# Attention's first unit on Trainium2: no strip moves, four tiles transposed on TensorE and taken off the bank by VectorE

## What is computed

```python
x = x + 0.5 * ffn(layernorm(x))
# attention of the middle part
q = layernorm(x) @ Wq.T + bq
scores = q @ memory_keys.T / sqrt(128)
probs = softmax(scores, axis=-1)
x = x + (probs @ memory_values) @ Wo.T + bo
x = x + 0.5 * ffn(layernorm(x))
```

## Time and profile before

| | |
|---|---|
| Median of 3 runs | 674.98 us (672.7 to 675.78) |
| The profiled execution | 673.04 us, span 671.4 us |
| PE, PEld busy | 613.3 us (91%), 432.9 us (64%) |
| DVE, ACT, POOL busy | 530.8 us (79%), 461.5 us (69%), 381.9 us (57%) |
| Mean granted clock of TensorE | 0.975 |
| DMA | 59.06 MB, strip moves: 480 issues |

### The profile page before, as it was taken

The page is one execution under the profiler, slowest core; times in us unless marked ns, Lnnn a source line. Parts: engine busy times, 40 slices in busy tenths (PEclk is TensorE's granted clock), DMA queues, the critical chain, the costliest instruction groups (busy, mean ns, idle before and its releaser), DMA issues.

```text
span 671.4 us, 9169 instructions
## 1 busy us (share of the span) xinstructions
PE 613.3 (91%) x2784; PEld 432.9 (64%) x2800; DVE 530.8 (79%) x968; ACT 461.5 (69%) x765; POOL 381.9 (57%) x378
## 2 busy tenths in 40 slices
PE   3888989669989999999999999999999987999997
PEld 2444434447667877778778778787787866645542
DVE  4889877858977887887897897897898765699885
ACT  3576777446667767777777786776776753577886
POOL 3856660035366766767687587586587783533100
PEclk9899999969998999999999999999999986999999
DMA  8021210043463553743734636527436320000000
GB/s 296 2 62 33 62 32 0 17 110 78 111 163 75 140 122 85 167 103 89 170 86 122 154 73 151 130 69 175 109 86 162 92 61 1 0 18 16 32 33 31
DMA packets 35555, 59.06 MB, mean 88 GB/s; under 512 B 8539, under 2 KB 9139, under 8 KB 35379
## 3 DMA queue, kind: packets, MB, share of 16 engines
q1 hardware_dynamic: 31891, 53.75, 31.8%
q10 hardware_dynamic: 3616, 4.73, 2.8%
HBM read 8.12 MB, written 2.10 MB: 15 GB/s over the span
## 4 chain that ended last, share of the span: by engine, by line
PE 62%; DVE 17%; issue 6%; ACT 4%; SPq 4%; POOL 3%; DMA 1%; ACTq 1%; DVEq 0%; POOLq 0%
PE banks L1244 7%; PE banks L1246 7%; PE banks L1245 7%; PE banks L1285 7%; PE banks L1286 6%; PE banks L1287 6%; PE banks L1264 4%; SPq L308 4%; PE banks L1120 4%; DVE probsT L895 3%; PE banks L1129 3%; DVE bank_max L998 3%; DVE E L993 3%; PE banks L1136 3%; PE banks L1295 2%
## 5 line engine op out<-in xcount | busy, mean ns | idle before, releaser
L460 POOL TENSOR_TENSOR p_lo<-probsT,p_hi 128x768 fp32r<-128x768 f32 (+1 forms) x128 | 226.7, 1776 | 174.7 <-ACT p_hi L652 174.5
L998 DVE TENSOR_REDUCE bank_max<-banks 128x1 f32<-128x1024 f32 x128 | 156.2, 1220 | 36.5 <-PE banks L1246 35.4
L652 ACT ACTIVATE p_hi<-probsT 128x768 fp32r<-128x768 f32 (+1 forms) x128 | 104.5, 816 | 22.9 <-PE banks L1287 18.9
L1244 PE MATMUL banks<-kv_lo,q_parts 128*128 128x512 f32 x256 | 112.6, 440 | 7.3 <-ACT E L670 4.8
L559 ACT ACTIVATE probsT<-probsT 128x1024 bf16<-128x1024 bf16 x96 | 92.2, 980 | 34.5 <-DVE probsT L895 31.6
L993 DVE STREAM_TRANSPOSE E<-E 128x1024 f32<-128x1024 f32 x92 | 113.6, 1234 | 2.1 <-ACT E L670 2.1
L895 DVE SCALAR_TENSOR_TENSOR probsT<-banks,E 128x1024 bf16<-128x1024 f32 x80 | 95.5, 1217 | 22.5 <-PE banks L1120 20.6
L1285 PE MATMUL banks<-p_hi,kv_lo 128*128 128x512 f32 x256 | 110.0, 430 | 2.5 <-POOL p_lo L460 2.1
L670 ACT ACTIVATE E<-banks,neg_max 128x1024 f32<-128x1024 f32 x92 | 102.4, 1113 | 7.4 <-DVE neg_max L1004 4.6
L644 ACT ACTIVATE p_hi<-banks 128x256 fp32r<-128x256 f32 (+1 forms) x128 | 52.3, 409 | 78.5 <-PE banks L1264 78.3
L1286 PE MATMUL banks<-p_lo,kv_hi 128*128 128x512 f32 x256 | 104.0, 406 | 0.0
(11 more groups left out here) (110 smaller groups left out, 880.3 us busy)
## 6 DMA issues: line engine op xcount, KB each, us to landing
probsT<-E SPq DMA_DIRECT2D x248, 128.0 KB, 2.4
probsT<-E SPq DMA_DIRECT2D x168, 64.0 KB, 2.0
E<-in_keys_values SPq DMA_DIRECT2D x8, 512.0 KB, 3.5
probsT<-E ACTq DMA_DIRECT2D x56, 64.0 KB, 2.4
out<-X SPq DMA_DIRECT2D x8, 256.0 KB, 2.1
X<-in_x SPq DMA_DIRECT2D x1, 1280.0 KB, 9.5
probsT<-E ACTq DMA_DIRECT2D x8, 128.0 KB, 4.1
X<-in_x SPq DMA_DIRECT2D x3, 256.0 KB, 5.6
```

The source lines that it names most:

```text
L460: pool.tensor_tensor(moved_part(p_lo, ring), moved_pair(ring // UP, ring % UP), moved_part(p_hi, ring).bitcast(fp32), ALU.subtract).then_i ...
L652: act.activation(moved_part(p_hi, ring), moved_pair(ring // UP, ring % UP), ACT.Copy).then_inc(moved_hi_done, 1)
L998: dve.tensor_reduce(bank_max[:, i % 2, h:h + 1], score_pair(u, i, h).rearrange("p b n -> p (b n)"), AX.X, ALU.max).then_inc(bank_max_done, 1)
L1244: pe.matmul(bank, qh, kl, start=True, stop=False)
```

## The change

Unit 0 moves no tile. Its four tiles' exponentials are written in plain order, two of them into the upper half of the arena probsT (`first_places`), two into probs. TensorE transposes one chunk of all four tiles into TB (`first_fill(m, 0)`), VectorE copies the bank to a new tile `taken` (`take_chunk(m, 0)`), TensorE fills the bank with the second chunk, and VectorE takes that too; the second take counts `p_lo_done`. ScalarE then makes one high part of all 16 quads of the pair, and GpSimd one low part. FIRST_LAG goes from 2 to 3, so unit 0's values come in steps 11 to 18 and its output projection in step 20. Fills run in steps 8 to 15, takes in steps 9 to 16, high parts in ScalarE's steps 7 to 14, low parts in GpSimd's steps 8 to 15. In steps 13 and 14, where the query takes its turn in TB, fill .0 stands behind the values. Moved tiles of later units go to the other half of probsT than before. The 32 moves of unit 0 are gone on both queues.

```diff
-FIRST_LAG = 2
+FIRST_LAG = 3
...
+        half_arena = MOVED * BLOCK
+        taken = arena[:, half_arena:half_arena + 4 * N].rearrange("p (r a c) -> p r a c", r=2, c=2 * SQ)
+        first_places = [arena[:, half_arena + (2 - t) * BLOCK:half_arena + (3 - t) * BLOCK] for t in range(2)]
...
-            return 2 if w in (0, LAST) else MOVED
+            return 0 if w == 0 else 2 if w == LAST else MOVED
...
-            for u in range(UNITS):
-                if u == 0:
+            for u in range(1, UNITS):
+                if u == 1:
...
             def moved_high(ring):
 
-                if ring % UP == 0:
+                if ring < UP:
+                    act.wait_ge(p_lo_done, ring + 1)
+                elif ring % UP == 0:
...
-                    if u == 0 and h == 5:
-                        act.wait_ge(z_done, GROUPS)
-                        act.wait_ge(down_done, GROUPS * SLOTS)
-                        act.wait_ge(squares_done, squares_of(1))
-                        for b in range(QUADS // 2, QUADS):
-                            for i in range(QUADS):
-                                move_strip(act, 0, 0, b, i)
...
+            def take_chunk(m, half):
+
+                dve.wait_ge(first_filled if half == 0 else probsT_done, m + 1)
+                wait(dve, moved_lo_done, m - 1)
+                dve.tensor_copy(taken[:, m % 2, :, half * SQ:(half + 1) * SQ],
+                                TB.rearrange("p (a q) -> p a q", q=SQ)
+                                ).then_inc(first_taken if half == 0 else p_lo_done, 1)
...
                     ring = pair_at(H + 1)
-                    if ring is not None:
+                    if ring is not None and ring >= UP:
                         own_low(ring)
+                    first = pair_at(H + 2)
+                    if first is not None and first < UP:
+                        take_chunk(first, 0)
                     if u < UNITS:
                         maximum(u, h // 2, h % 2)
                         if h % 2 == 1:
                             negative_maximum(u, h // 2)
+                    if first is not None and first < UP:
+                        take_chunk(first, 1)
...
+            def first_fill(m, half):
+
+                if half == 0:
+                    pe.wait_ge(exp_done, 2 * GT - 1 if m < UP // 2 else 2 * GT)
+                    wait(pe, p_lo_done, m)
+                    if m == 0:
+                        pe.wait_ge(expz_done, GROUPS)
+                        pe.wait_ge(weighted, GROUPS * SLOTS)
+                else:
+                    pe.wait_ge(first_taken, m + 1)
+                c = 2 * m + half
+                for t in range(GT):
+                    last = pe.transpose(TB[:, t * P:(t + 1) * P], own_exponentials(0, t)[:, c * P:(c + 1) * P],
+                                        ident[:, :])
+                last.then_inc(first_filled if half == 0 else probsT_done, 1)
...
                     filled = pairs_until(H + 2)
+                    first = pair_at(H + 3)
+                    if first is not None and first >= UP:
+                        first = None
+                    takes_turn = prepares and h in (Q_HALF, Q_HALF + 1)
+                    if first is not None:
+                        filled = pairs_until(H + 3)
+                        if not takes_turn:
+                            first_fill(first, 0)
...
                     ring = pair_at(H + 2)
-                    if ring is not None:
+                    if first is not None or ring is not None and ring >= UP:
...
-                        transpose_pair(ring)
+                        if first is None:
+                            transpose_pair(ring)
+                        else:
+                            if takes_turn:
+                                first_fill(first, 0)
+                            first_fill(first, 1)
```

## The result

The change makes the kernel slower: 699.37 us (697.6 to 700.9, 4 runs) against 674.29 us (672.7 to 675.78, 4 runs), a ratio of 1.0379 with a 95% interval of 1.035 to 1.0409. The forecast was 688, with a range to 699. The sign and the round trip were right, the size was about 10 us short. The profiled execution has a span of 697.0 us against 671.4.

A forecast was written before the change was run, and what follows sets the result against it. The prediction took TensorE's own work to bound the kernel in steady state. Its terms summed to +11.4 us at full clock, plus 3.7 for the clock: +15.1 on the profiled 673.04 us gave 688 us, range 680 to 699.

The forecast's parts named there:

- the round trip: Steps 8 to 15: scores, maximum, second take, then fill; the fill starts 3.55 us into a step, 2.1 us TensorE idle.
- Steps 0 to 8, gain 1.6: Unit 0's four VectorE square transposes go, so step 8's scores start at 131.5 against 133.07: 1.6 us gained.
- The moves of unit 0: Before step 9: without strip moves ScalarE's 7.40 us go; first fill at 134.3, 7 us earlier than before's first transposes.
- The new chain: Steps 8 to 15: fills wait for takes, ordinary steps 5.8 us against 3.25; step 16 starts 12.9 us later.
- The clock: TensorE's clock in the new idle holes: steps 9 and 10 at half clock, +3.7 us; steps 11 to 15 full.
- the clock rival: Clock at half through all of steps 11 to 15: 5 x 3.0 us more, 703 us; chance 0.15.
- of 3.5 us some 2.7 come back: Unit 2's late strip moves: SyncE's queue is idle when unit 2 comes, returning 2.7 us; bounds 0 and 3.5.
- The later values and projection: FIRST_LAG 3 puts unit 0's last values into step 18, +0.9 us, and its projection a step later, +0.3 us.
- Faster: Rival: the takes are hidden and fills cost only their issue, -4 us, giving 669 us; chance 0.05.
- no change: Rival: takes cost 0.3 us, all late waits return, before's half-clock steps are saved: 674 us; chance 0.04.
- The longer chain: Rival: ScalarE's high part delays exponentials and scores, each step gaining another 1 to 2 us: 698 us; chance 0.10.

The follow-up runs named there:

- the interleaved kernel: The changed kernel with VectorE's order as take m.1, maximum, take (m+1).0, square transpose: 677.51 us, ratio 1.0057 to the kernel before.
- both takes first: The changed kernel with VectorE doing both takes of a pair ahead of the step's maximum: 681.32 us in one run, span 679.4 us.

## Why the prediction was wrong in size

- **Steps 0 to 8, gain 1.6: mis-sized a little.** T(8) - T(0) was 19.29 and is 18.14, a gain of 1.15.
- **The moves of unit 0: right.** ScalarE's gap is gone, the exponentials of step 6 start at 134.48, the first fill at 135.74, both some 0.5 us later than forecast once the 0.91 us by which this execution's attention starts late (114.69 against 113.78) is taken off.
- **The new chain: right, and shown.** Waits of 2.0 to 2.2 us in front of the fills, with the take as releaser; at full clock steps of 5.91 for 5.8, 8.40 for 8.5. The take was 0.68 us, at the upper of the two rows that bounded it and not at 0.62, which is under 0.1 us a step. The full-clock lengths were short too, by 1.2 us: with the clock held at 1.00, steps 9 to 15 took 45.3 where the forecast had 44.1. Undoing the order alone took away 17.6 us of span.
- **The clock, "steps 9 and 10 at half clock with their fills: +3.7" and, of steps 11 to 15, "I leave them at full clock": this is the step that failed.** The clock also fell in steps 11, 13 and 15. The runs put it at about 8.5 us (2.6 in steps 9 and 10, 5.9 in 11 to 15), 4.8 more than the term. The prediction's own sign for the clock rival, scores spaced 0.43, was there in step 11 and not in step 12. I had a row for each answer, a hole of 2.20 us that kept the clock and one of 1.78 that lost it, and settled on the better one for five steps in a row. The clock fell in three of the five. The Trainium skill (TensorE: Matmul & The Clock Gate, A second HAM failure mode) tells of small idles between groups of matmuls that make the clock swing between its two levels; the trace agrees, with the granted clock at 0.56, 1.00, 0.66, 1.00 and 0.82 in stretches of one region. The rival that stood on it gave 703 for half clock in all five steps; 5.9 of its extra 15 us came.
- **Steps 16 to 27, "of 3.5 us some 2.7 come back": wrong, by 1.4 us.** They took 37.5 us against 37.6, where I had 36.1. The later values and projection, +0.9 and +0.3, were right in sum: steps 18 to 21 took 1.3 us more. What came back at steps 26 and 27 was 1.4 us and not 2.7. The premise was that SyncE's queue was still at unit 1's strips. It was not, and the kernel before could have said so. Its queue stood idle for unit 2's squares (first the queue's wait between 179 and 186 us, then two rows of the timeline):

```profile
SPq L357 <- DVE E L993: 6.0, 1, 6.0
...
183.90 1.23 DVE L993 STREAM_TRANSPOSE E<-E 128x1024 f32<-128x1024 f32 x1
...
185.21 1.29 SPq L308 DMA_DIRECT2D probsT<-E  x2
```

  From 185.21 to the exponentials at 199.65 are 14.4 us. In the changed kernel the queue issued its last strip of unit 1 at 196.4 and the first of unit 2 at 210.87, as unit 2's squares ended, and the exponentials of step 24 still stood for the landing:

```profile
209.56 1.24 DVE L1012 STREAM_TRANSPOSE E<-E 128x1024 f32<-128x1024 f32 x1
...
210.87 17.41 SPq L321 DMA_DIRECT2D probsT<-E  x26
...
225.23 1.11 ACT L688 ACTIVATE E<-banks,neg_max 128x1024 f32<-128x1024 f32 x1 [2.98 <-DMA probsT<-E]
...
226.49 0.50 PE L1268 MATMUL banks<-kv_lo,q_parts 128*128 128x512 f32 x1 [1.91 <-ACT E L688]
```

  The bound was from unit 2's squares to the landing, again 14.4 us for 16 strips, and it came along with those squares. Only the clock's fall behind it (1.5 us in step 27 before) went away. I take that for luck of the execution, which is not shown: it is there again in the interleaved kernel (4.59) and not with both takes first (3.06).
- **What is left over: 2.4 us outside steps 0 to 28**, 0.9 before and 1.5 after. The kernels of the experiments differ there by as much; I did not look for a cause.
- **Faster, and no change:** did not happen. Their point of decision, the take ahead of the scores' end, was put in by experiment, and only with ScalarE's help did it reach parity.
- **The longer chain:** did not happen. In steps 9 to 15 TensorE stood in front of fills and of the query's turn, with takes as releaser, and never in front of scores.

The sum by measured sizes: -1.15 (steps 0 to 7) + 24.40 (8 to 15) - 0.11 (16 to 27) + 2.4 = 25.6 us, the difference of the spans. The forecast had -1.6, +18.1 and -1.5. The 10.5 us between the two are 4.8 of the clock, 1.4 of full-clock lengths (1.2 in steps 9 to 15, 0.2 in step 8), 0.5 in steps 0 to 7, 1.4 in steps 16 to 27 and 2.4 outside.

## What to carry to other kernels

Before handing a bank back and forth between two engines, write down where each engine's queue stands when the bank comes free. A copy that stands behind an op that needs the producer's newest work turns a hand-over of 0.7 us into a round trip of 3.6 us, and moving it one place is worth more than what the change was made for. Where a change leaves a hole in every step of TensorE, price the steps at half clock and at full clock and put the forecast between them, not at the better end. And before counting on an earlier queue to end a stall, look whether that queue is busy at all: here the transfer waited for the unit's own data, before and after.

## What the runs showed that I had not expected

More work made the kernel faster: 64 products that nobody reads took 7.3 us off steps 8 to 15 (11.3 off the span, in one execution), at a clock of 1.00 where it had been 0.80 from 138 to 190 us:

```profile
138.00:190.00 52.00, 33.55 (x129) 24.57 (x128) 25.37 (x32) 15.03 (x21) 19.08 (x15) 0.80 0.18 41
```

In the order with no single hole over about 1.6 us the same filler cost what it gave back. And a plain fp32 copy off the bank by VectorE took 0.65 to 0.69 us for 512 columns, hardly less than a subtraction with a second operand (0.69) and more than ScalarE's copy of the same bank (0.60).
